# Graph attention over a sparse adjacency: when the first layer's row gathers are issued

## The reference

```python
def layer(x, adj, W, a):              # four of them, with their own W, a
    Wh = x @ W
    e = (Wh @ a[:64, 0])[:, None] + (Wh @ a[64:, 0])[None, :]
    e = leaky_relu(e)                 # slope 0.2, 0.01, 0.2, 0.01
    scores = where(adj > 0, e, -huge)
    return softmax(scores, axis=1) @ Wh   # + bias in layer 1, elu in the others
for l in range(4):
    x = layernorm(x + layer(x, adj, W[l], a[l]))
```

## Time and profile before

| | |
|---|---|
| timed runs, median (lowest, highest) | 926.0 us (925.73, 931.46) |
| the profiled execution | span 935.2 us, first to last instruction |
| instructions | 11216 |
| busy: PE, DVE, ACT, POOL | 407.2, 379.7, 400.7, 381.1 us |
| gathers (L395) | 340, of 965 ns mean |
| mean granted TensorE clock | 0.771 of full |

### The profile page before, as it was taken

One profiled execution on the slowest core, in us unless ns is written; L12 is line 12 of the kernel. 1 busy time (PEld: TensorE's weight loads), 2 busy tenths in 40 slices (PEclk: granted clock), 3 DMA queues, 4 the chain that ended last, 5 costly groups with the idle time before them and its releaser, 6 DMA issues.

```text
span 935.2 us, 11216 instructions
## 1 busy us (share of the span) xinstructions
PE 407.2 (44%) x3613; PEld 363.3 (39%) x3625; DVE 379.7 (41%) x1697; ACT 400.7 (43%) x861; POOL 381.1 (41%) x396
## 2 busy tenths in 40 slices
PE   2555232221469972001099833002499620020994
PEld 1444222121459862001098723001498520010974
DVE  3898666332417960000038810000179500000498
ACT  2939886674148830001068600001389300010685
POOL 0313676757710017777300057776000177772000
PEclk9999999999869975555589955555699655555998
DMA  8948999982100001111000011211000012110000
GB/s 326 420 173 342 425 391 321 337 315 69 20 9 1 24 28 26 27 27 28 13 2 14 24 27 27 28 27 27 0 1 25 28 27 27 28 28 12 1 19 32
DMA packets 21109, 87.07 MB, mean 93 GB/s; under 512 B 6836, under 2 KB 10999, under 8 KB 16695
## 3 DMA queue, kind: packets, MB, share of 16 engines
q1 hardware_dynamic: 10022, 73.70, 19.9%
q0 software_dynamic: 10880, 11.51, 8.3%
q10 hardware_dynamic: 144, 1.08, 0.3%
HBM read 80.90 MB, written 5.37 MB: 92 GB/s over the span
## 4 chain that ended last, share of the span: by engine, by line
another core or an unknown queue 23%; PE 20%; issue 17%; DVE 8%; ACT 6%; POOL 1%; DMA 1%; ACTq 0%; POOLq 0%
PE bank L554 6%; PE bank L580 6%; PE bank L567 4%; ACT arena L722 3%; PE bank L455 3%; ACT xt L646 1%; POOL xg L395 1%; DVE key L1034 1%; DVE arena L1007 1%; PE bank L551 1%; ACT arena L713 1%; PE bank L446 1%; DVE stats L1059 1%; DVE key L1043 0%
## 5 line engine op out<-in xcount | busy, mean ns | idle before, releaser
L395 POOL DMA_INDIRECT xg<-table,index x340 | 328.1, 965 | 366.8 <-DMA table<-wh 265.2
L713 ACT ACTIVATE arena<-bank,sloped_own 128x256 f32<-128x256 f32 (+3 forms) x144 | 76.9, 536 | 410.6 <-remote 222.4
L1007 DVE CUSTOM_DVE_ANT_0 arena<-bank,arena 128x256 f32<-128x256 f32 (+3 forms) x144 | 71.6, 498 | 408.1 <-issue 226.0
L554 PE MATMUL bank<-packed,xg 128*128 128x128 f32 x744 | 127.3, 312 | 54.2 <-DMA xg<-table,index 52.9
L669 ACT ACTIVATE arena<-arena,half 128x4096 bf16<-128x4096 int32 x32 | 117.9, 3704 | 49.0 <-remote 29.5
L551 PE MATMUL bank<-penalty,ident_b 128*128 128x256 bf16 (+2 forms) x132 | 43.5, 329 | 215.1 <-DVE seg_max L1007 127.6
L551 PEld LDWEIGHTS bank<-penalty,ident_b 128*128 128x128 bf16 x144 | 19.2, 134 | 271.8 <-issue 219.1
L554 PEld LDWEIGHTS bank<-packed,xg 128*128 128x128 f32 x744 | 119.2, 227 | 3.2
L567 PE MATMUL bank<-packed,arena 128*128 128x128 f32 x372 | 71.4, 303 | 75.8 <-ACT arena L731 70.3
L580 PE MATMUL bank<-xg,arena 128*128 128x64 f32 x744 | 100.6, 271 | 0.0
L580 PEld LDWEIGHTS bank<-xg,arena 128*128 128x128 f32 x744 | 93.2, 192 | 4.0
(11 more groups left out here) (101 smaller groups left out, 576.1 us busy)
## 6 DMA issues: line engine op xcount, KB each, us to landing
arena<-in_adj_t SPq DMA_DIRECT2D x32, 2048.0 KB
xg<-table,index POOLq DMA_INDIRECT x340
table<-wh SPq DMA_DIRECT2D x24, 132.0 KB, 1.7
table<-wh ACTq DMA_DIRECT2D x1, 1056.0 KB, 12.8
x<-in_x SPq DMA_DIRECT2D x1, 1024.0 KB, 11.1
out_x<-x SPq DMA_DIRECT2D x8, 128.0 KB, 1.9
slot_row<-in_c_slot_row SPq DMA_DIRECT2D x1, 768.0 KB, 11.6
packed<-in_c_packed SPq DMA_DIRECT2D x1, 343.0 KB
```

The source lines that it names most:

```text
L395: pool.indirect_dma_start(out=xg[:, c, :], out_offset=None, in_=table[l][:, :], in_offset=bass.IndirectOffsetOnAxis(ap=index[:, c:c + 1], ...
L554: t = nc.tensor.matmul(bank[:, c * P:(c + 1) * P], tcol_wide(xg[:, c1 + c, TCOL:TCOL + 1]), ident[:, :], start=False, stop=(c == m - 1))
L713: nc.scalar.activation(score[:, n % RING, 0:m * P], score_ps[n % len(score_ps)][:, 0:m * P], ACT.Relu, bias=sloped_own[:, k:k + 1], scale= ...
L1007: nc.vector.tensor_tensor_reduce(out=y, in0=score_ps[n % len(score_ps)][:, 0:m * P], in1=y, scale=1.0, scalar=MASKED, op0=ALU.add, op1=ALU ...
```

## The change

GpSimd issues no gather while the adjacency is read. Behind the last `slot_rows` it waits for the table and issues all 85 gathers in one burst, in the order of chunks as before, with one wait on `index_made` at the first chunk of each batch. The two constants and the helper that shared the gathers out are gone. Nothing changes on the other engines, nor in layers 1 to 3.

```diff
-GATHER_START = 3
-GATHER_SHARE = 3
...
-            def gather_some(count, made):
-                for c in range(started[0], min(started[0] + count, FIRST[BATCHES[made][0]] if made < len(BATCHES) else NCH)):
+            def gather_all():
+                for c in range(NCH):
                     k = TILES_OF_CHUNK[c][0]
-                    b = [b for b, (k0, n) in enumerate(BATCHES) if k0 <= k < k0 + n][0]
-                    if started[0] == 0 or c == FIRST[BATCHES[b][0]]:
-                        pool.wait_ge(index_made, b + 1)
+                    for b, (k0, n) in enumerate(BATCHES):
+                        if c == FIRST[k0]:
+                            pool.wait_ge(index_made, b + 1)
                     gather(0, k, c)
-                    started[0] += 1
-            started = [0]
             pool.wait_ge(loaded, 16 * NLOAD)
             for b in range(len(BATCHES)):
-                if b == GATHER_START:
-                    pool.wait_ge(written, 16)
                 if b >= 1:
                     slot_rows(b - 1)
                 columns(b)
-                if GATHER_START <= b < len(BATCHES) - 1:
-                    gather_some(GATHER_SHARE * BATCHES[b][1], b - 1)
             slot_rows(len(BATCHES) - 1)
-            gather_some(NCH, len(BATCHES) - 1)
-            gather_some(NCH, len(BATCHES))
+            pool.wait_ge(written, 16)
+            gather_all()
```

## The result

The kernel after takes 987.9 us (median of 4 runs, 987.24 to 988.36) against 928.4 us for the kernel before in the same comparison: a ratio of 1.065, 95% interval 1.062 to 1.068. Forecast were 983.1 us and +57.1; measured are 987.9 and +59.5. Half of the 4.8 us between the two times is the base, which was taken as 926.0.

A forecast was written before the change was run, and what follows sets the result against it. TensorE's work and signals were taken to come late while GpSimd issues gathers. A gain of 33.1 us before the burst and a cost of 90.2 in layer 0 took 926.0 to 983.1 us, range 968.7 to 1002.0.

The forecast's parts named there:

- Stage: Adjacency stage and tail: without gathers, 5.0 us a tile, and the burst starts 33.1 us earlier, at 205.3.
- The floor of the transfer: Adjacency stage: the first masks, waiting for the adjacency's DMA, come every 4.87 us; 5.0 was taken, near that.
- the waits for nothing visible: Adjacency stage: VectorE's 56.4 us of "remote" waits, put down to gathers; none forecast before its first look at codes.
- Layer 0: Layer 0 gets a full burst of 85 gathers and lasts 198.3 us in place of 108.1: +90.2 us.
- The sum: Whole kernel: -33.1 us before the burst and +90.2 in layer 0 make +57.1, so 983.1 us.
- layers 1 to 3: The later layers: claimed unchanged, with periods of about 198 us.
- TensorE's work and its signals come late as long as GpSimd issues gathers: Adjacency stage and layers: assumed cause of the waits, such as VectorE starting on codes 11.3 us late.
- the gather at 218.99: Adjacency stage: its 0.94 us was read as showing that VectorE work beside a gather doesn't slow it.
- Rival 1: Adjacency stage: only the moved gathers' transfer time, 15.1 us, comes back; 1001.1 us in all; chance 0.10.
- Rival 2: Adjacency stage: it doesn't shorten at all, as VectorE or ScalarE takes over; 1016.2 us; chance 0.05.
- Rival 3: Layer 0: work runs beside its burst, 128.2 us, +20.1 in place of +90.2; 913.0 us in all; chance 0.04.

The follow-up runs named there:

- filler: The kernel after, with GpSimd kept busy by memsets, without DMA, where the six moved trains of gathers had stood: 999.9 us, 1.068 times before.
- plain: The kernel after, with 66 plain 128 x 256 byte DMAs from SyncE among the adjacency loads of tiles 14 to 30: 999.9 us, 1.068 times before.
- second group: Runs on a chip where the kernel before took 930.1 us; the kernel after, run there again unchanged, took 986.5 us, ratio 1.062.
- third group: Three runs with added waits, on a chip where the kernel before took 699.9 us: 774.1, 725.7 and 804.0 us.
- window run: The kernel after, with GpSimd waiting after a tile's second gather until the previous tile's have landed: 725.7 us against 699.9, ratio 1.038.
- fifth-gather run: The kernel after, with GpSimd waiting in all four layers after every fifth gather until it has landed: 823.0 us, 0.886 times before.

## Why the prediction was right

*Stage.* Forecast: last mask at 193.4, burst at 205.3, gain 33.1. Measured in the profile: 194.5, 205.8, 32.6. The floor of the transfer (4.87 us a tile) plus a little was the right reading. That the waits for nothing visible would go with the gathers is shown by the profile after. That neither GpSimd's occupation nor the packets alone are the main part is shown by the filler and plain runs: 7.1 and 7.5 us at most. Even added up they leave 18 of the 32.6 us; that these come from the issuing of gathers itself is what is left, not what a run shows.

*Layer 0.* Forecast: 198.3 us, as in the layers beside it; measured 194.3. The term was 4.0 us too large. Layers 1 and 2 themselves vary by about half of that from one execution to another (196.3 us in the profile after, 198.3 before). But layer 0 took 194.3 us in the second group as well, so its 4.0 us are hardly scatter; no run looked for their cause. What the 86.2 us consist of only the third chip tells, and across chips: there a layer with its full burst and no lateness took 130.5 us, so about 22 us are the burst's own length and about 64 the lateness.

*The sum.* In the profiled executions it is +50.0 and in the timed runs +59.5; the forecast, +57.1, lies between. Against the profiles the forecast is 7.1 us too high: 4.0 for layer 0 and 3.6 for layers 1 to 3, which I took as unchanged and which are that much shorter in the profile after, less 0.5 for the stage. The 9.5 us between profiles and timed runs are that the profiled span of before is 6.8 us over the median of its runs (928.4), while that of the kernel after is 2.7 under its own. So that the timed difference comes within 2.4 us of the forecast is in part luck: the profiles don't settle the sum better than to some 10 us.

*What the steps said of the cause.* "TensorE's work and its signals come late as long as GpSimd issues gathers" was right as far as it decides this change, and too simple. First, it takes an unbroken row: trains of 4 cost the stage 0.15 us a gather, trains of 12 cost 0.49 (32.6 / 66). Second, in the layers a pause until the gathers have landed all but ends it, and a bound on how many are under way does not. Third, it isn't seen on every chip. One reading in the prediction doesn't bear what was built on it: the gather at 218.99, taken as one beside VectorE's work, stands in VectorE's own wait of 11.72 us. Other rows of the kernel before do show it: the gather at 135.13, beside VectorE's unbroken work from 134.04 on, takes 0.94 us too.

*The rivals.* Rival 1 (only the transfer time comes back, 15.1 us) is refuted: the gain was 32.6, and the plain transfers cost 7.5. Rival 2 (no gain) too. Rival 3 (layer 0 runs beside its burst, 128.2 us, result 913) was wrong for the chips of the comparison. On the chip of the third group its layer is what was measured: 130.5 us. But the sign wasn't the rival's there either. The window run, which is the kernel after with a wait that made no measurable difference to the kernel before, is 25.8 us slower than before on that chip. A layer 0 of 130.5 us in place of 108.1 makes 22.4 of it, so by this estimate nothing is left of the 33.1 us of gain. That would fit a gain that comes only from ending a lateness that this chip doesn't show, but it isn't shown: no profile of the kernel before was taken there.

*What stays open.* Why TensorE's signals come late in an unbroken row of gathers, and why one of the chips is free of it, no run tells. I didn't run the kernel after itself on that chip, nor trains of ten on one that has the lateness, so how it grows between trains of five and of twelve is not known.

## What to carry to other kernels

Gathers issued by GpSimd can cost more than their own time: look at what the other engines do beside them, and where waits for "issue" and "remote" coincide with them, suspect the gathers. Before moving gathers into one burst, or before leaving them in one, try short trains with a wait for the landing of the last; here, behind the load stage, that beat both kernels by 11% and 17% on a chip that has the lateness. Keep such waits out of a stage that saturates the DMA engines, where one took up to 9.1 us. And measure on several chips: where the lateness is absent, the kernels with waits were 11% (every tenth) and 15% (every fourth and fifth, with gathers in the stage) slower than the kernel before, where the window run, nearly the move of the gathers alone, was 4% slower.

## What the runs showed of the hardware

- The same kernel took 926 to 936 us in four comparisons and 699.9 us in a fifth, on a chip with no "remote" wait in any of the three profiles taken there. A difference of 25% between chips for one program was not expected, and it decides what is worth tuning. That it belongs to the chip is argued from one group of runs on one such chip.
- A gather of 128 rows took GpSimd 0.94 us and 1.25 us with its gap, with 264 bytes a row and with 64.
- The wait for the landing of a gather just issued cost GpSimd 30.1 / 16 = 1.9 us in the fifth-gather run, behind the adjacency, and 59.8 / 11 = 5.4 us beside it in the run with two gathers per tile.
- Beside a burst of 85 gathers the other engines' late starts recur at the same distances on two chips (14.00 and 25.20 us in both profiles of the kernel after and in the plain run); with a wait after every fifth gather no wait of ScalarE in layer 0 for nothing visible is over 3.1 us.
